# The ends of two program blocks: a barrier on semaphores in place of the one with GpSimd's drain, and the semaphores of three stages cleared together

## What is computed

```
x = x + retention(conditioned(x))            # 16 heads, causal decay
gate, experts of cond2:  top 2 of 8 experts, three matrix layers each
gate, experts of ffn:    top 2 of 8 experts, two matrix layers each
x = x + experts_ffn(experts_cond2(x))
```

```
x = x + _L0_attn_ref(_L0_cond_ref(x, cond_256, cond_64, ...), ...)
x = x + _L0_ffn_ref(_L0_cond2_ref(x, cond_256[:, None, :], ...), L0_ffn_w_gate, ...)
x = x + _L1_attn_ref(_L1_cond_ref(x, cond_256, ...), ...)
x = x + _L1_ffn_ref(_L1_cond2_ref(x, cond_256, ...), ...)
```

## Time and profile before

| | us |
|---|---|
| median of 3 runs | 2144.31 |
| lowest, highest | 2141.67, 2149.12 |
| the profiled execution, its own time | 2129.55 |
| its span, from the first to the last instruction | 2127.4 |

### The profile page before, as it was taken

How to read it: one execution, slowest core, us unless ns; L and a number is a source line. 1 busy time by engine, 2 the same in 40 slices (tenths; PEclk the granted TensorE clock), 3 DMA queues, 4 the chain that set the end, 5 groups by cost and what they waited for, 6 DMA issues and landing times. The chain is left out here.

```text
span 2127.4 us, 37418 instructions
## 1 busy us (share of the span) xinstructions
PE 1743.6 (82%) x12063; PEld 1248.1 (59%) x12063; DVE 1289.3 (61%) x3359; ACT 1061.4 (50%) x3153; POOL 872.8 (41%) x1091
## 2 busy tenths in 40 slices
PE   2288845995449957999959899999999999899887
PEld 1144424985349844565638677777777777555533
DVE  6668752454624557787747566656665665456556
ACT  0044312442124316788824566666666666666543
POOL 0034564654746523244335864151516060622233
PEclk9999757997569978999979999999999999999988
DMA  9300013333112242000013222121121212110001
GB/s 395 135 2 11 22 35 87 108 87 97 62 56 72 65 151 70 26 30 25 25 53 82 57 68 64 48 54 48 53 56 46 56 46 55 54 49 28 24 11 40
DMA packets 155793, 135.77 MB, mean 64 GB/s; under 512 B 88037, under 2 KB 128166, under 8 KB 153446
## 3 DMA queue, kind: packets, MB, share of 16 engines
q1 hardware_dynamic: 144230, 98.03, 16.0%
q0 software_dynamic: 9088, 18.70, 2.8%
q10 hardware_dynamic: 2304, 16.91, 1.9%
HBM read 77.03 MB, written 56.54 MB: 63 GB/s over the span
## 5 line engine op out<-in xcount | busy, mean ns | idle before, releaser
L2683 DVE TENSOR_TENSOR delta_sv<-delta_sv,delta_zp 32x256 f32<-32x256 f32 x384 | 161.3, 420 | 165.9 <-PE delta_zp L2324 159.2
L825 POOL DMA_INDIRECT y<-moe_y,moe_aim x156 | 176.6, 1132 | 160.2 <-DVE moe_y L965 68.0
L2596 POOL TENSOR_TENSOR delta_dd<-delta_ll,delta_minus 128x1024 f32<-128x1024 f32 (+1 forms) x9 | 24.9, 2770 | 383.3 <-DMA delta_ll<-lanes 383.2
L1778 ACT ACTIVATE field_p<-field_sp,field_nm 128x128 f32<-128x128 f32 x512 | 179.9, 408 | 0.9 <-DVE field_nm L1862 0.8
L2603 POOL TENSOR_TENSOR delta_dd<-delta_dd,delta_prod 128x30 f32<-128x30 f32 (+11 forms) x270 | 152.4, 565 | 21.2
L2601 POOL TENSOR_TENSOR delta_prod<-delta_ll,delta_dd 128x30 f32<-128x30 f32 (+11 forms) x270 | 138.3, 512 | 21.2
L2324 PE MATMUL delta_zp<-delta_sv,delta_ct 128*32 128x128 f32 x1536 | 122.0, 280 | 20.7 <-DVE delta_sv L2683 12.9
L2292 PE MATMUL delta_xp<-delta_la,delta_di 128*128 128x256 f32 x512 | 123.3, 396 | 13.0 <-DMA delta_di<-inverses 6.8
L1778 ACT ACTIVATION_READ_ACCUMULATOR field_p<-field_sp,field_nm 128x1 f32 x512 | 127.6, 249 | 0.0
L2292 PEld LDWEIGHTS delta_xp<-delta_la,delta_di 128*128 128x128 f32 x512 | 98.6, 197 | 38.3 <-issue 25.4
L2324 PEld LDWEIGHTS delta_zp<-delta_sv,delta_ct 128*32 128x32 f32 x1536 | 70.1, 109 | 84.5 <-DVE delta_sv L2683 51.1
(11 more groups left out here) (547 smaller groups left out, 4594.2 us busy)
## 6 DMA issues: line engine op xcount, KB each, us to landing
delta_al<-alpha SPq DMA_DIRECT2D x33, 512.0 KB, 4.2
pairs<-c_none ACTq DMA_DIRECT2D x16, 1032.0 KB, 16.7
moe_xg<-pairs SPq DMA_DIRECT2D x78, 129.0 KB, 2.2
moe_yt<-y SPq DMA_DIRECT2D x16, 512.0 KB, 4.3
w_E<-in_E_dram SPq DMA_DIRECT2D x1, 4624.0 KB, 21.9
w_E<-in_E_dram SPq DMA_DIRECT2D x8, 578.0 KB, 4.2
lanes<-delta_la SPq DMA_DIRECT2D x128, 32.0 KB, 1.7
delta_di<-inverses SPq DMA_DIRECT2D x64, 64.0 KB, 2.3
```

The source lines that it names most:

```text
L825: nc.gpsimd.indirect_dma_start(results, bass.IndirectOffsetOnAxis(ap=aim[:, t % AR, j:j + 1], axis=0), y[:, t % YS, j, :], None).then_inc( ...
L1778: last = nc.scalar.activation(p[:, slot, h, :], s_ps[i][:, k, :], ACT.Exp, bias=nm[:, slot, h:h + 1], accum_out=zs[:, slot, h:h + 1])
L2683: nc.vector.tensor_tensor(sv[rows, two, :], sv[rows, two, :], z_ps[2 * pair // HH][rows, at, :], ALU.subtract).then_inc(s["z_kept"], 1)
```

## The change

`Memory` gets two more arguments. With `kept` it no longer clears its semaphores and no longer runs the second barrier at release: it appends its semaphores to the list `kept`. With `earlier` it starts its own list with those. The retention and the first experts are given `kept=c["sems"]`, the second experts `earlier=c["sems"]`. And the blocks of the retention and of the first experts are opened with `no_gpsimd_drain=True`.

```diff
-    def __init__(self, nc, ctx, stage):
-        self.nc, self.ctx, self.stage, self.sems = nc, ctx, stage, []
+    def __init__(self, nc, ctx, stage, earlier=(), kept=None):
+        self.nc, self.ctx, self.stage, self.sems, self.kept = nc, ctx, stage, list(earlier), kept
         ctx.callback(self.release)

     def release(self):
-        self.nc.clear_and_free_semaphores(self.sems)
-        self.nc.all_engine_barrier()
+        if self.kept is None:
+            self.nc.clear_and_free_semaphores(self.sems)
+            self.nc.all_engine_barrier()
+        else:
+            self.kept.extend(self.sems)
...
-        m = Memory(nc, ctx, "ret")
+        m = Memory(nc, ctx, "ret", kept=c["sems"])
...
-        with nc.Block() as block:
+        with nc.Block(no_gpsimd_drain=True) as block:
...
-        m = Memory(nc, ctx, "moe1")
+        m = Memory(nc, ctx, "moe1", kept=c["sems"])
...
-        with nc.Block() as block:
+        with nc.Block(no_gpsimd_drain=True) as block:
...
-        m = Memory(nc, ctx, "moe2")
+        m = Memory(nc, ctx, "moe2", earlier=c["sems"])
...
-    w, c = {"raw_dram": I["raw"]}, {}
+    w, c = {"raw_dram": I["raw"]}, {"sems": []}
```

## The result

The changed kernel takes 2132.63 us (median of 20 runs, 2122.57 to 2137.72) against 2139.76 us of the kernel before in the same session (20 runs): a ratio of 0.9967, 95% interval 0.9953 to 0.9980, which is 7.1 us faster (4.3 to 10.0). In the first of them one execution of nine took 2284.56 us at a granted clock of 0.798, and the ratio leaves it out. The mean of the three is 0.9958, some 9 us. The forecast was 11.9 us.

A forecast was written before the change was run, and what follows sets the result against it. Bound by what arrives last at each barrier, POOL's Drain at two block ends, and the way to the next work. -10.90 - 1.5 + 0.53 = -11.9 us, so 2144.3 - 11.9 = 2132.4 us, range 2124 to 2141.

The forecast's parts named there:

- The two Drains: POOL's Drains at the retention's and first experts' ends, 5.29 and 5.61 us, go from the only running chain: 10.90 us saved.
- the two second barriers: Second barrier with second Drain and clear at both ends goes: 0.7 and 0.8 us, together 1.5 us saved.
- The clear: At the second experts' end it covers 125 semaphores in place of 27: some 710 ns, 0.53 us added in full.
- The cover at the second experts' end: POOL's Drain there may grow, up to 20.5 us, yet ends 11 us before SP comes: counted as 0.
- The 4 ns a transfer: Drain length per indirect transfer, from the two removed Drains: 284 transfers would cost some 0.8 us more than 78.
- What POOL has behind it in the next stage: Drain work going on beside the first experts' start would end at 339.5, before POOL's first instruction at 348.9: hidden by 9 us.
- The clock: PE's restarts from the lower clock after both ends: taken as 0, with 1 us either way each, and 1 us for later restarts.
- the 5.3 us come back: Rival: the Drain's time is POOL's own work and still delays the barrier; only 1.0 us gained, 2143.3 us; chance 0.05.
- Slower scatters: Sign in the first experts: scatters stay at a mean of 0.99 us; growth by a fifth would prove the prediction wrong.
- Half of it given back by a later restart or load: Rival: PE's restart or a first load falls worse in both stages; about 6 us gained, 2138.3 us; chance 0.04.
- The median against the profiled execution: Three-run median lies 14.8 us above the profiled execution; the same 11.9 us was taken off both.
- The rule on the Drain: The skill's rule that a drain waits for full idleness puts the 5.3 us on POOL; the rows couldn't tell.

The follow-up runs named there:

- after_again: The changed kernel again, unaltered, for a second profile and more times: 2117.75 us against 2127.07 for the kernel before, ratio 0.9955.
- drain_kept: The changed kernel with POOL's Drains given back at both block ends, the second barriers and clears still gone: 2127.25 us, ratio 0.9998 to the kernel before.
- ret_only: The changed kernel with the Drain left out at the retention's end alone, given back at the first experts' end: 2128.72 us, ratio 0.9997 to the kernel before.
- drain_beside: The changed kernel with a Drain put first in POOL's code of the first and second experts' blocks: 2119.52 us, ratio 0.9963 to the kernel before.
- ret_only_again: An unchanged copy of ret_only, measured again in another session: 2137.37 us, ratio 0.9991 to the kernel before.
- the three measurements of after: The changed kernel measured in three sessions, unaltered: ratios 0.9967, 0.9955 and 0.9952 to the kernel before.
- drain_twice: drain_beside with a second Drain right behind the first in POOL's code of the first experts: 2119.61 us, one execution only.
- first_experts_only: The changed kernel with the Drain left out at the first experts' end alone, given back at the retention's end: 2123.18 us, ratio 0.9982 to the kernel before.
- before_again: The kernel before, an unchanged copy, for a second profile: 2140.0 us, ratio 1.0001 to the kernel before.

## Why the prediction was right, and where it was off

**The mechanism and its terms.** The two Drains: forecast 10.90 us, and with the two second barriers 12.4. Measured at the holes of before and after_again, both without stalls: 9.79 to 3.82 and 9.95 to 3.49, which is 5.97 + 6.46 = 12.4 us. By itself a second barrier is worth 0.7 to 0.8 (drain_kept), the rest is the Drain. Right to a tenth. The sentence under it, that no other engine takes POOL's place because POOL is last by more than 13 us, holds for the retention's end everywhere, but at the first experts' end only where DVE has no stalls: with them SP is last, and the hole there is 4.3 to 4.4 us in place of 3.5.

**The clear** was forecast at some 710 ns and took 716. The step was mis-sized by what stands in front of it: POOL's short Drain ahead of the clear takes 248 ns where it took 106. That could have been read in before, where this Drain grows with the clear behind it: 106 ns for 27 semaphores, 118 for 46, 175 for 83. From the start of DVE's last step of the second experts to the field's first load it is 4.51 us in place of 3.85, so some +0.65 and not +0.53.

**The cover at the second experts' end.** Forecast: at most 20.5 us for the Drain, some 10.4 expected, and 0 for the time. It took 11.60: a mis-sized 2.0 us of growth in place of 0.8, and hidden as said (over at 782.8, SP at 803.3). The 4 ns a transfer, which the 0.8 was worked out from, fails: 64 transfers more left the Drain of ret_only at 5.62 us, and 220 or 284 make no difference at the last one.

**What POOL has behind it in the next stage** is hidden: drain_beside puts the whole 5.3 us there and 5.6 us at the next, at no cost that shows.

**The clock** is the term that failed. I took 0 with 3 us to either side, and looked for it only at the restarts behind the holes. It acts in whole stages. The eight profiles without the Drain at the retention's end have a mean of 239.3 us for the retention (ret_only_again less its stall), the six with it 237.9: 1.4 us. In the first experts' matmuls the means are 152.6 and 151.1: 1.5 us. So 12.4 - 0.65 - 1.4 - 1.5 = 8.9 us, and the three measurements of after say 9. That is no proof of the sum. Its last two terms are means over patterns of the clock that differ by up to 4.5 us for the same code (retention 237.6 to 242.1), and it leaves out the 1325 us behind the second experts. From the field's first load to the end the same two groups have means of 1328.8 and 1327.4 us, with single profiles between 1324.9 and 1331.4; with that 1.4 us too the sum would be 7.5. What the runs show is a loss of some 3 us between the ends and the total, and a scatter of the stages by the clock that is large enough for it. I don't claim that the change causes it; the cause stays open.

**The rivals.** That the 5.3 us come back is refuted: SP is released 0.3 us after POOL's branch. Slower scatters: 998 and 992 ns against 994, refuted. Half of it given back by a later restart or load: a part of this did happen, by other ways, the 0.8 us at each end in two of four sessions and the clock.

**The median against the profiled execution.** I took the 14.8 us between them as something that the removed work doesn't depend on. That held. The likely cause of the difference is the stalls at line 141: before's profile has none, and the three runs belong to a session in which the profile of after has them. No profile of the kernel before was taken in that session, so this is inferred. The predicted 2132.4 us meets the 2132.63 us that were measured partly by luck. The kernel before was 2139.76 in that session and not 2144.3, and the gain was 7.1 and not 11.9; the two differences nearly cancel.

**The rule on the Drain.** drain_twice bears on the sentence of the Trainium skill, page "PSUM — Partial Sum Buffer", section "Engine vs sequencer instructions", that a drain waits for the engine to go fully idle. By it the second Drain finds POOL idle and takes no time, and it took 34 ns: they agree. Whether POOL would come to an end by itself in those 5.3 us, or the Drain sets the work going, isn't settled, but the rows speak for the second. In the eight profiles with a Drain there it starts 2.56 to 2.93 us after the start of the last scatter, and it takes 5294 ns in every one. A wait for work that was under way already would have been shorter where it began later. A Drain put some 10 us behind the last transfer would tell, and it wasn't tried.

**Not settled.** The two ends don't add up. ret_only gained 0.06% and first_experts_only 0.17% (means of two measurements), both together 0.42%. Each mean is uncertain by about 0.1%, and each of the two kernels has the 0.04% of the second barriers in it, so the missing 0.2%, some 4 to 5 us, is at the edge of what the measurements allow. In the profile of ret_only the clock is slow (239.6 and 154.7 us, the long value in both columns), but that execution wasn't slow as a whole. In the profile of ret_only_again it isn't the clock: up to the field's first load that one is 3.3 us ahead of before_again, and 5.8 us without its longer stalls (14.1 us in all against 11.7), and then it loses 3.1 us to it in the field, the delta and the last layer, in a part of the program that all the kernels have alike.

## What to carry to other kernels

Where a block's end comes right behind indirect transfers on GpSimd, look for its Drain between the last landing and the release: here it was 5.3 to 5.6 us in which nothing ran, twice. A barrier without it took the time off the path, and the Drain could be paid beside later work, and the order of the data is kept by the waits for landings that the program has in front of the barrier (GpSimd's for the scatters, SyncE's for the results). The total here gave some 9 us of the 12 found at the two places: compare lengths stage by stage over several profiles of the same kernel before a difference of 1 to 5 us is put down to the change.

## What the runs showed of the hardware

- A Drain on GpSimd behind indirect transfers took 5294 ns in all six profiles that had it at the retention's end, and in the two that had it right behind (64 transfers), 5.6 us at the first experts' end (behind 142 transfers, or behind 206), 9.6 us at the second experts' (78) and 11.6 us there when the one before it was left out (220 or 284). The last two include some 3 us in which the stage's last transfers are still run. Right after another Drain it takes 34 ns.
- SP's first assert behind the retention's end took 33 and 29 ns with the Drain ahead of it and 700, 348 and 979 ns without it, in the same kind of session; in the other sessions it took 29 or 33 ns either way.
- An instruction that clears a range of semaphores took 178 ns for 27, 283 for 46, 483 for 83 and 716 for 125, and the short Drain ahead of it 106, 118, 175 and 248 ns.
- The same code of the retention on the same data, with the clock's first rise anywhere between 115.2 and 118.5 us, takes 237.6 to 242.1 us.
- In some sessions DVE stands still for 4.8 to 7.6 us ahead of one and the same instruction, twice in every execution that was profiled there. No wait or transfer in the trace explains it.
